# One core, gated delta rule and top-2 expert layer: the output gate in one ScalarE step, all five engine lists in another order, and unread TensorE products in three places

## The reference, cut to what matters

```python
mixed = conv4(einsum('bth,ch->btc', hidden, qkv_w))      # q, k, v: 3 x 8 heads x 128
z     = einsum('bth,vh->btv', hidden, z_w)
beta, alpha = sigmoid(b), exp(-exp(A_log) * softplus(a + dt_bias))
# per token: S = S*alpha;  S += k (v - k.S) beta;  o = q.S
o = o * rsqrt(mean(o*o) + 1e-6) * norm_w
o = o * (z * sigmoid(z))                                 # the output gate
x = x + o @ out_w.T
x = x + experts(layernorm(x))                            # router, top 2 of 8, relu, two products
```

## Time and profile before

| | us |
|---|---|
| three runs, median (lowest to highest) | 1408.25 (1407.96 to 1409.8) |
| profiled execution, its own time | 1407.17 |
| its span, first to last instruction | 1405.3 |
| mean clock granted to TensorE, of full speed | 0.933 |
| busy in the span: TensorE / VectorE / ScalarE / GpSimd | 1172.5 / 1167.0 / 834.4 / 710.7 |
| the 15 like stages, 137 to 1163 us | 1026 |

### The profile page before, as it was taken

One profiled execution on the slowest core, in us unless ns is written; L12 is line 12 of the kernel. 1 busy time (PEld: TensorE's weight loads), 2 busy tenths in 40 slices (PEclk: granted clock), 3 DMA queues, 4 the chain that ended last, 5 costly groups with the idle time before them and its releaser, 6 DMA issues.

```text
span 1405.3 us, 33741 instructions
## 1 busy us (share of the span) xinstructions
PE 1172.5 (83%) x11978; PEld 944.4 (67%) x11978; DVE 1167.0 (83%) x2531; ACT 834.4 (59%) x2536; POOL 710.7 (51%) x598
## 2 busy tenths in 40 slices
...
DMA packets 163174, 97.07 MB, mean 69 GB/s; under 512 B 115623, under 2 KB 148269, under 8 KB 161988
## 3 DMA queue, kind: packets, MB, share of 16 engines
...
## 4 chain that ended last, share of the span: by engine, by line
DVE 32%; PE 26%; POOL 16%; issue 10%; DMA 7%; ACT 6%; SPq 2%; POOLq 0%; DVEq 0%; ACTq 0%
POOL kq L637 9%; DVE Y_sb L1056 7%; DVE blkT L1060 7%; PE kx L1541 3%; POOL decay L629 3%; POOL rows_in L609 2%; DMA blkN<-scr_n 2%; PE kx L1636 2%; POOL kq L620 2%; PE rc L1703 2%; DVE blkN L1047 2%; DVE Gs L1204 1%; DVE area L1146 1%; ACT Gs L836 1%; PE rc L1704 1%
## 5 line engine op out<-in xcount | busy, mean ns | idle before, releaser
L637 POOL TENSOR_TENSOR kq<-tapA,area 128x256 f32<-128x256 f32 x256 | 253.2, 1003 | 89.1 <-DVE area L1146 88.1
L758 ACT ACTIVATE area<-pj,taps 128x256 f32<-128x256 f32 x256 | 123.3, 482 | 138.8 <-PE pj L1555 130.4
L1056 DVE TENSOR_TENSOR Y_sb<-blkT,blkN 128x4 f32<-128x4 f32 (+18 forms) x304 | 172.4, 567 | 10.5
L1541 PE MATMUL kx<-kq 128*128 128x128 f32 x1024 | 143.1, 288 | 43.2 <-ACT area L767 32.6
L609 POOL DMA_INDIRECT rows_in<-rowbuf,dest x64 | 64.8, 1012 | 214.8 <-DVE dest L1132 187.3
L1541 PEld LDWEIGHTS kx<-kq 128*128 128x128 f32 x1024 | 130.2, 199 | 57.8 <-issue 41.2
L1143 DVE SCALAR_TENSOR_TENSOR tapA<-pj,taps,tapA 128x256 f32<-128x256 f32 x256 | 122.2, 477 | 51.7 <-ACT tapA L758 49.8
L620 POOL TENSOR_TENSOR kq<-kq,area 128x1024 f32<-128x1024 f32 x64 | 151.1, 2363 | 0.0
L1060 DVE TENSOR_REDUCE blkT<-Y_sb 128x2 f32<-128x4 f32 (+18 forms) x304 | 142.5, 469 | 5.2
L758 ACT ACTIVATE tapA<-pj,taps 128x256 f32<-128x256 f32 x256 | 123.1, 481 | 0.0
L1146 DVE SCALAR_TENSOR_TENSOR area<-pj,taps,area 128x256 f32<-128x256 f32 x256 | 121.4, 474 | 0.0
...
...
## 6 DMA issues: line engine op xcount, KB each, us to landing
...
scr_n<-area SPq DMA_DIRECT2D x128, 32.0 KB, 1.6
...
```

Source lines behind the costliest of these rows:

```text
L637: nc.gpsimd.tensor_tensor(dst[:, n % H, :], tapA[:, n % RING, :], tapB[:, n % RING, :], ALU.add).then_inc(conv_done, 1)
L758: ins = nc.scalar.activation(dst[:, n % RING, :], pj[n % 2][:, k:k + GT], ACT.Copy, scale=taps[:, t, k:k + 1])
L1056: ins = nc.vector.tensor_tensor(p4, bc(blkT[:, r0:, j:].rearrange("p r (o m) -> p r o m", o=1), [128, nr, w, wd]), bc(blkN[:, j:j + w, j:] ...
L1541: ins = mm(o, lhs[:, hh, cs], rhs_[:, hh, cs], start=True, stop=True)
```

## The change

Three things are done at once.

The gate: ScalarE's `zt` now computes silu(z) in one step instead of tanh, with the scale 1/WSCALE, and signals `zg_ready` itself; VectorE's `zg` step (L1176) is gone from the text and from the code, and the constant folded into the output weights changes from 0.5/WSCALE/VSCALE to 1/VSCALE. Since `zt` now writes the finished gate, it waits until `g` of the group before has read the old one.

The order: `ORDER` is another text. Every step but `zg` is still there.

Unread products: a table STAND_INS names three places in TensorE's list, ahead of ktr.1.1, kq.0.1 and z.1.0, at which 4, 6 and 9 products of 128x512 (fp16) are written to a bank that is free (pj1, pj1, kx0) and that nobody reads. They are emitted only in the 15 like stages.

```diff
-         ka_ready, aq_ready, z_mm, z_tanh, zg_ready) = sems(
+         ka_ready, aq_ready, z_mm, zg_ready) = sems(
...
-            first.14 inv.0 taps.15 ks.1.1 last.13 rhs.1.0 inv.1 inv.2 last.14 inv.3 inv.4 first.15 rhs.1.1 u.1.0 inv.5
+            last.12 taps.14 g.0.0 bi st.0.1 scale.0 proj.15 v.1.0 first.14 taps.15 first.15 inv.0 ktr.0.0 o.0.1 inv.1 inv.2
...
                     elif step == "zt":
                         c, u = arg
+                        if g is not None:
+                            act.wait_ge(g_ready, halves(g, c, u))
                         act.wait_ge(z_mm, halves(a, c, u))
-                        nc.scalar.activation(zg[:, c, HU * u:HU * u + HU, :], heads(pj[u]), ACT.Tanh,
-                                             scale=0.5 / WSCALE).then_inc(z_tanh, 1)
+                        nc.scalar.activation(zg[:, c, HU * u:HU * u + HU, :], heads(pj[u]), ACT.Silu,
+                                             scale=1.0 / WSCALE).then_inc(zg_ready, 1)
...
-                    elif step == "zg":
-
-                        c, u = arg
-                        dve.wait_ge(z_tanh, halves(a, c, u))
-                        nc.vector.scalar_tensor_tensor(out=half(zg, c, u), in0=half(zg, c, u), scalar=1.0,
-                                                       in1=heads(pj[u]), op0=ALU.add, op1=ALU.mult).then_inc(zg_ready, 1)
-
...
+            STAND_INS = {
+                ("ktr", 1, 1): (("z", 0, 1), pj[1], 4),
+                ("kq", 0, 1): (("z", 0, 1), pj[1], 6),
+                ("z", 1, 0): (("gt", 0, 0), kx[0], 9),
+            }
+
...
+            def stand_in(step, g, a, r):
+
+                use, bank, n = STAND_INS[step]
+                bank_free(use, g, a, r)
+                for _ in range(n):
+                    mm(bank[:, :], wv_hi[:, 0, 0:C], wv_hi[:, 0, 0:512], start=True, stop=True)
...
                 for step, *arg in STEPS:
+                    if g is not None and a is not None and (step, *arg) in STAND_INS:
+                        stand_in((step, *arg), g, a, r)
```

More of the change, by code:

```diff
@@ L249, in preln_delta_moe_kernel @@
         ORDER = """
-            proj.0 proj.1 taps.0 taps.1 diag.0 first.0 v.0.0 proj.2 m.1.0 taps.2 al.0 first.1 proj.3 m.0.0 last.0 taps.3
-            rdiag.0 me.1.0 v.0.1 first.2 proj.4 first.3 ka.0 last.1 me.0.0 m.1.1 taps.4 proj.5 me.1.1 ks.0.0 m.0.1 taps.5
-            scan.0 first.4 m.1.2 proj.6 me.0.1 rdiag.1 ks.0.1 last.2 last.3 first.5 me.1.2 proj.7 m.0.2 m.1.3 al.1 taps.6
-            diag.1 first.6 taps.7 last.4 proj.8 first.7 kk.0.0 me.0.2 me.1.3 m.0.3 last.5 proj.9 last.6 xl.0 rhs.0.0 me.0.3
@@ L254, in preln_delta_moe_kernel @@
-            last.7 sp.0 scan.1 nm.0.0 taps.8 kk.0.1 u.0.0 taps.9 aq.0 nm.0.1 kk.1.0 first.8 last.8 nm.1.0 kk.1.1 nm.1.1
-            proj.10 ue.0.0 rhs.0.1 taps.10 o.0.0 first.9 proj.11 first.10 proj.12 u.0.1 taps.11 first.11 taps.12 last.9
-            sd.0.0 proj.13 ktr.0.0 ue.0.1 first.12 xl.1 aq.1 last.10 no.0 no.1 sq.0.0 proj.14 taps.13 last.11 st.0.0 ac.0
-            sd.0.1 taps.14 g.0.0 o.0.1 first.13 ka.1 st.0.1 sq.0.1 proj.15 last.12 v.1.0 sm v.1.1 scale.0 bi ks.1.0 kd.0.0
-            first.14 inv.0 taps.15 ks.1.1 last.13 rhs.1.0 inv.1 inv.2 last.14 inv.3 inv.4 first.15 rhs.1.1 u.1.0 inv.5
@@ L259, in preln_delta_moe_kernel @@
-            kq.0.0 u.1.1 ue.1.0 g.0.1 inv.6 ue.1.1 o.1.0 o.1.1 ktr.0.1 sq.1.0 inv.7 s2 ac.1 sd.1.0 sp.1 sq.1.1 kd.0.1 inv.8
-            scale.1 inv.9 inv.10 at.0.0 inv.11 ktr.1.0 inv.12 g.1.0 last.15 kd.1.0 inv.13 rms.0 inv.14 sd.1.1 ktr.1.1 kd.1.1
-            rms.1 gn.0.0 kq.0.1 gn.0.1 gt.0.0 inv.15 at.0.1 z.0.0 inv.16 gt.0.1 gte.0.0 nr g.1.1 xt inv.17 gte.0.1 z.0.1
-            zt.0.0 xe lg out.0 gn.1.0 zt.0.1 inv.18 rk gn.1.1 gt.1.0 inv.19 gt.1.1 x2.0 inv.20 gte.1.0 inv.21 kq.1.0 gte.1.1
-            pf out.1 zg.0.0 z.1.0 tp zt.1.0 zg.0.1 ps st.1.0 z.1.1 zt.1.1 zg.1.0 zg.1.1 xs.0 x2.1 to at.1.0 kq.1.1 at.1.1 ti
@@ L264, in preln_delta_moe_kernel @@
-            st.1.1 xs.1 tj sc
+            ka.0 proj.0 taps.0 proj.1 first.0 v.0.0 proj.2 al.0 taps.1 m.0.0 taps.2 m.1.0 first.1 proj.3 taps.3 rdiag.0
+            diag.0 first.2 v.0.1 xl.0 first.3 scan.0 me.0.0 proj.4 proj.5 me.1.0 last.0 last.1 taps.4 taps.5 diag.1 m.1.1
+            me.1.1 first.4 first.5 ks.0.0 m.0.1 last.2 me.0.1 last.3 al.1 proj.6 taps.6 last.4 last.5 m.1.2 proj.7 rdiag.1
+            ks.0.1 me.1.2 m.0.2 m.1.3 first.6 last.6 taps.7 first.7 scan.1 last.7 kk.0.0 proj.8 me.0.2 me.1.3 nm.0.0 taps.8
@@ new lines, in preln_delta_moe_kernel @@
+            first.8 m.0.3 proj.9 me.0.3 aq.0 kk.0.1 kk.1.0 proj.10 nm.0.1 kk.1.1 taps.9 first.9 last.8 nm.1.0 last.9 rhs.0.0
+            ka.1 proj.11 sm taps.10 nm.1.1 ac.0 u.0.0 rhs.0.1 first.10 taps.11 sp.0 first.11 u.0.1 ue.0.0 proj.12 proj.13
+            o.0.0 s2 taps.12 no.0 first.12 ue.0.1 taps.13 sd.0.0 first.13 no.1 proj.14 st.0.0 last.10 last.11 sd.0.1 sq.0.0
+            last.12 taps.14 g.0.0 bi st.0.1 scale.0 proj.15 v.1.0 first.14 taps.15 first.15 inv.0 ktr.0.0 o.0.1 inv.1 inv.2
+            sq.0.1 inv.3 last.13 ks.1.0 inv.4 inv.5 v.1.1 inv.6 rhs.1.0 sp.1 kd.0.0 ks.1.1 rhs.1.1 u.1.0 inv.7 inv.8 g.0.1
```

13 lines of the change are left out of this document (9 added, 4 removed).

## The result

The changed kernel takes 1433.72 us (median), the kernel before 1409.03 beside it: ratio 1.0176, 95% interval 1.0159 to 1.0194. It is slower. The forecast was 1387, the range 1366 to 1420. The profiled execution took a span of 1435.9, 30.6 more than the 1405.3 of before. Of these, 23.3 lie between the first and the last step on blkN, 1.3 ahead of them and 6.0 behind.

The account below looks back on a forecast made before the run. No single engine was the bound but a stage-to-stage loop through GpSimd, TensorE, VectorE and DMA trips. 31.1 + 0.3 + 22.6 + 13.0 = 67.0 against 68.4, -1.4 a stage over 15 stages, gave 1387 us, range 1366 to 1420.

Parts of the forecast that it names:

- the cut of the loop: One stage's chain cut into inverse 31.1, zg 1.3, ps to last.7 22.2, last.7 to blkN 14.0: together 68.6 us.
- zg to x2.0, -1.0 a stage: Ahead of ps, two zg (1.3) leave VectorE and x2.0 (0.3) stands there instead: -1.0 us a stage.
- the table loads: Two more on ScalarE, in the first stage and ahead of the expert layer's exponential: 0.5 us taken for both.
- The inverse, 31.1: VectorE's inverse: shorter by first.15, x2.0 and rk's wait, but 3.8 lost to GpSimd instead of 2.0; 31.1 as before.
- `ps` to `last.7`, 22.6: GpSimd's stretch, ka.0 now ahead of diag.0: 22.2 + 0.4 = 22.6 us, bounds 22.0 to 24.5.
- the middle: End of the inverse to end of nm.1.1: 26.9 us by the forecast.
- `last.7` to blkN, 13.0: 14.0 less 0.6 on TensorE and 0.4 for asking for ac.0 earlier: 13.0 us, bounds 12.3 to 14.0.
- Two `zg` behind `ps`, 0: Between ps and the next stage's first taps VectorE would wait instead, so removing them gains 0.
- The unread products: On TensorE, 4.1 us a stage; fill gaps, hold the clock, gt.0.0 some 1 us late, ps with 0.9 to spare.
- Clock 1.00 through the whole stage: Expected in the changed kernel's profile: TensorE's clock stays up, no slice at 0.5.
- Rival 1: Late last.0 holds taps.4, and merge steps behind it on ScalarE: +0.4 to +1.6 a stage, 1414 to 1432; chance 0.16.
- Rival 4: Clock falls all the same, 4.4 us at half clock stay, TensorE late: stage 68.1, 1404; chance 0.04.

Follow-up runs that it names:

- t_products: Kernel before with the one-step gate, old order and 25 unread products, six of them ahead of proj.2 and m.1.0: 1402.8 us, ratio 0.9954.
- zg_products: Kernel before with tanh and zg kept, plus 25 unread products: 1400.1 us, ratio 0.9927.
- gate_alone: Kernel before with only the gate made in one step; old order, no unread products: 1416.4 us, ratio 1.0056.
- rows_wait: gate_alone with GpSimd issuing the four row DMAs only when the inverse has been written to DRAM: 1433.6 us, ratio 1.0177.
- pool_start_old: Changed kernel with the first seven steps of GpSimd's list in the order of before: about 7 us less than the changed kernel.
- merge_first: Changed kernel with me.1.1 and me.0.1 ahead of taps.4 and taps.5 in ScalarE's list: 1481.9 us, ratio 1.0536.
- mixed: Changed kernel with GpSimd's and SP's old lists, but xs.0 behind ti, and eight more unread products: 1397.0 us, ratio 0.9902.

## Why the prediction was wrong

The step that failed is the cut of the loop. I read from the chain of one stage that everything from the end of the inverse to `last.7` runs through `zg`, `ps` and GpSimd, and took every us on it as one of the loop. Two branches leave the end of the inverse. The other is the writing out and reading back of T, the taps, `scan.0` and the merge. It was as long to within about 0.5 a stage (t_products against zg_products), and in the changed kernel it is the one that ends last: from the end of the inverse to the end of `nm.1.1` it takes 29.7, where the forecast had 26.9 for the first branch. I had used it two paragraphs later, to put the other two `zg` at 0, and did not ask what it does to the first two.

Point by point:

- *zg to x2.0, -1.0 a stage.* Wrong: gate_alone is 7 us slower, zg_products is level with t_products. Worth about 0.5. What the table loads cost on the path is not told apart by any run, so neither is the price that the Trainium skill gives them (ScalarE: Activation LUTs, What ACT_TABLE_LOAD costs): three loads of 1.28 stand in the changed kernel's list (one before), and the last part of the span, 283.5 before, is 283.9 in rows_wait, 284.7 in zg_products, 285.2 in t_products, 287.9 in gate_alone and 289.5 in the changed kernel. The two pairs that differ by the gate (before and rows_wait, which also has one wait more; zg_products and t_products) are 0.4 and 0.5 apart, but gate_alone has the same loads and is 4.3 above before, so no price follows. Where the 6.0 of the changed kernel come from is open. The sum in the prediction was off too: two loads at the 2.66 of that page are, as an estimate, 5.3, which is 4.8 more than the 0.5 taken and not 2.5.
- *The inverse, 31.1.* Right, 31.0, and mostly for the reason given: `rk` waits in 2 of its 16 places instead of in all (19.7 us before, 8.3 now), the multiplies with both inputs in the big memory are 36.2 longer in all at L1057 and 14.3 shorter at the two lines of the earlier trace rows and its neighbour (L1048 and L1044 are at 0.69): +1.4 a stage, forecast +1.8.
- *`ps` to `last.7`, 22.6.* The term that was mis-sized, with its neighbour: the middle was to shrink by 1.2, zg included, and grew by 1.6. I gave ka.0 ahead of diag.0 0.4. pool_start_old shows 7 us in all for the order of the first seven steps. The contest with `scan.0` itself is hardly longer than before (3.9 on average, 3.7 before), but the scan begins a us later (12.1, not 11.0) and so ends 1.3 later, and with it first.4 and all behind it. The half clock that follows in 10 stages was no term of the sum at all.
- *`last.7` to blkN, 13.0, ac.0 ahead of the blocks as a gain of 0.4.* Not a gain: from nm.1.1 it is 9.2 against 8.9, and SP's list put back wins 6 us once GpSimd's is.
- *Two `zg` behind `ps`, 0.* It fits: first.0 waits 2.82 for ScalarE's taps in the stage shown. No run took these two out by themselves.
- *The unread products.* Their timing was right to a few tenths: gt.0.0 has no wait ahead of it, and `ps` waits 5.7 us in all for `pf`. "Clock 1.00 through the whole stage" was wrong. It stays up where they stand and falls where TensorE waits next, for T.
- *Rival 1* gave 1414 to 1432 at a chance of 0.16 and is nearest. Its sign for itself came true: in the stage shown the kk stands behind m.0.3 (712.14 + 1.07) and not behind `last.7`. Its cause only half. Late `last.0`, yes. But the merge was held on TensorE, in the chain above, by the projection that waits for first.4 behind `scan.0`; for merge steps held on ScalarE merge_first shows nothing.
- *Rival 4* took a fall at the old place. It came at a new one. Filling the waits there was worth 9 us in the old order and nothing in the new.

The Trainium skill's sentence on the shared port pair (SBUF — State Buffer, SBUF: two separate sides: "an exclusive lock, not a bandwidth split") fits the rows above: 4.60 and 5.46 for a scan of 2.28, and four `last` in 4.81 behind it.

What each part is worth, by differences of medians, each good to some 5 us: gate +7; its unread products in the old order -4; GpSimd's start +7, GpSimd's tail +7 (about 2 a stage in the inverse, most of it given back at ac.0), SP's list +6. The three new lists that are left may be worth something with the clock held up: mixed is 3 us below the best of the old order, but the intervals overlap, and it also has xs.0 behind ti and two more unread products than those.
